# A depthwise-conv tile shared by two engines: GpSimd's 16 taps and VectorE's nine kept as two sums, value weights folded into the projection

## What is computed

```python
# block 1: linear attention over raw and convolved q, k, v
qkv = concat(h @ wq.T, h @ wk.T, h @ wv.T)            # 768 channels
dw  = depthwise_conv5x5(qkv, dw_kernel)               # 25 taps for each channel
pw  = grouped_conv1x1(dw, pw_kernel)                  # groups of 8 channels
f   = concat(qkv, pw).reshape(B, 64, 3 * 8, N)        # 64 heads of 8
query, key, value = relu(f[:, :, :8]), relu(f[:, :, 8:16]), f[:, :, 16:]
scores = einsum('bhdn,bhen->bhde', concat(value, 1), key)
out = einsum('bhde,bhen->bhdn', scores, query); out = out[:-1] / (out[-1:] + EPS)
x   = batchnorm(conv1x1(out, proj_kernel)) + x
# block 2: softmax attention over the 1024 pixels of each image
norm = (x - mean) / sqrt(var + EPS)
att  = softmax((f_w norm + f_b)^T (g_w norm + g_b))   # 1024 x 1024
x    = o_w (att applied to (h_w x + h_b)) + o_b + x
```

## Time and profile before

| what | value |
|---|---|
| median of 3 runs | 716.86 us (716.64 to 716.91) |
| the profiled execution: its own time | 716.49 us |
| its span, first to last instruction | 714.5 us |
| instructions in the span | 8764 |
| mean granted TensorE clock | 0.969 |
| one image in the middle | 153.9 us |

### The profile page before, as it was taken

One profiled execution on the slowest core, in us unless ns is written; L12 is line 12 of the kernel. 1 busy time (PEld: TensorE's weight loads), 2 busy tenths in 40 slices (PEclk: granted clock), 3 DMA queues, 4 the chain that ended last, 5 costly groups with the idle time before them and its releaser, 6 DMA issues.

```text
span 714.5 us, 8764 instructions
## 1 busy us (share of the span) xinstructions
PE 647.9 (91%) x3236; PEld 484.4 (68%) x3236; DVE 567.7 (79%) x661; ACT 470.0 (66%) x744; POOL 541.2 (76%) x253
## 2 busy tenths in 40 slices
PE   4979989999999999899999999899899946997998
PEld 3845458656767887657687886658678833485887
DVE  5899998879989999888899999888899982442221
ACT  4795529788676967978686697977688552232231
POOL 4999979899989998899989998999999790000000
PEclk9999999999999999999999999999999986898999
DMA  8000010001100000001100000000100000000000
GB/s 291 1 1 1 0 33 28 0 1 59 60 1 16 15 31 1 1 0 60 60 6 25 17 16 1 0 1 6 54 16 16 31 0 0 1 0 1 15 15 30
DMA packets 6538, 16.25 MB, mean 23 GB/s; under 512 B 864, under 2 KB 992, under 8 KB 5984
## 3 DMA queue, kind: packets, MB, share of 16 engines
q1 hardware_dynamic: 6496, 15.69, 6.0%
HBM read 11.50 MB, written 4.19 MB: 22 GB/s over the span
## 4 chain that ended last, share of the span: by engine, by line
PE 50%; DVE 19%; ACT 14%; POOL 12%; issue 4%; DMA 1%; POOLq 0%; SPq 0%; DVEq 0%; ACTq 0%
PE ps L614 13%; POOL rows L1318 12%; PE ps L590 12%; DVE ps L1107 11%; ACT prod L873 5%; PE ps L691 5%; PE ps L625 3%; PE ps L605 3%; DVE small L1244 2%; PE ps L739 2%; PE ps L533 2%; PE ps L456 1%; PE ps L665 1%; ACT kt L887 1%; ACT rows L1015 1%
## 5 line engine op out<-in xcount | busy, mean ns | idle before, releaser
L1318 POOL TENSOR_TENSOR conv<-conv,prod 128x930 f32<-128x930 f32 (+4 forms) x197 | 433.1, 2232 | 30.7 <-ACT prod L873 27.4
L1107 DVE SCALAR_TENSOR_TENSOR ps<-raw,dw_sb,ps 128x930 f32<-128x930 f32 (+4 forms) x295 | 354.1, 1200 | 7.7
L873 ACT ACTIVATE prod<-raw,dw_sb 128x930 f32<-128x930 f32 (+4 forms) x233 | 252.1, 1136 | 30.7 <-POOL conv L1318 18.1
L614 PE MATMUL ps<-ht,pt 128*128 128x256 f32 x512 | 115.1, 379 | 0.0
L614 PEld LDWEIGHTS ps<-ht,pt 128*128 128x128 f32 x512 | 95.1, 190 | 11.8
L1318 POOL TENSOR_TENSOR rows<-rows,prod 128x930 f32<-128x930 f32 (+4 forms) x36 | 83.0, 2306 | 14.1 <-ACT prod L873 9.3
L1015 ACT ACTIVATE rows<-ps,small 128x1024 f32<-128x1024 f32 x32 | 35.6, 1113 | 76.9 <-DVE small L1248 76.9
L1244 DVE TENSOR_REDUCE small<-ps 128x1 f32<-128x1024 f32 x32 | 39.0, 1220 | 33.0 <-PE ps L590 33.0
L590 PE MATMUL ps<-hi,t_hi 128*128 128x512 f32 x128 | 46.2, 444 | 13.1 <-ACT rows L1015 13.1
L887 ACT ACTIVATE kt<-ps 128x256 f32<-128x256 f32 x68 | 31.5, 466 | 23.4 <-PE ps L647 19.6
L590 PE MATMUL ps<-lo,t_hi 128*128 128x512 f32 x128 | 43.1, 420 | 0.0
(11 more groups left out here) (137 smaller groups left out, 1046.4 us busy)
## 6 DMA issues: line engine op xcount, KB each, us to landing
q_raw<-x_dram SPq DMA_DIRECT2D x8, 512.0 KB, 6.4
x<-x_dram SPq DMA_DIRECT2D x4, 1024.0 KB, 4.8
out_dram<-x_t SPq DMA_DIRECT2D x16, 256.0 KB, 2.3
conv<-wqkv_dram SPq DMA_DIRECT2D x1, 768.0 KB, 4.5
conv<-fg_dram SPq DMA_DIRECT2D x1, 512.0 KB, 5.3
proj_sb<-proj_dram SPq DMA_DIRECT2D x1, 512.0 KB, 7.5
pw_sb<-pw_dram SPq DMA_DIRECT2D x1, 384.0 KB, 6.4
mask_sb<-masks_dram SPq DMA_DIRECT2D x1, 264.0 KB, 6.1
```

The source lines that it names most:

```text
L614: mm = pe.matmul(dst[:, 0:C], pt[:, i % PT_BUFS, j, :], ht[:, j, :], start=(j == 0), stop=(j == NB - 1))
L873: act.activation(dst, view, ACT.Copy, scale=weight(t, i)).then_inc(prod_ready, 1)
L1107: return dve.scalar_tensor_tensor(dst, view, w, before, ALU.mult, ALU.add)
L1318: pool.tensor_tensor(total, total, product, ALU.add).then_inc(conv_pool, 1)
```

## The change

- POOL's part of tile 1 becomes one sum in `conv`: taps 0 to 15 (0 to 20 in the first image). The first seven stand among tiles 4 and 5, the last nine are the late ones. So tap 0 goes to `conv`, and there is no product into a row buffer.
- DVE's part becomes a sum of its own: taps 16 to 24 (21 to 24), starting with a plain product, the last tap writing to row buffer 2, now called `dve_part`. That tap waits for the transposes of the last softmax row in that buffer. DVE no longer waits for POOL's sum.
- PE multiplies `dve_part` first, then, after POOL's last add, `conv`.
- ACT may make three late products while the softmax loop of the last image still ends (`LATES_ATT`). The product buffers are counted through from image to image; before, the first five products of an image waited for all adds of the image before it.
- The pointwise weights of the value tiles are multiplied once, at the start, into the projection weights (two products on PE, one copy on ACT), and the value tiles of the key/value blocks are transposed instead of multiplied. The kernel's host side lays these weights out transposed, in the same array.
- The tables are written anew; POOL splits the second image's input after its early adds and not among them.

Line numbers in the changed kernel differ by some 10 to 20: L873 is L890, L1318 is L1336, L1107 is L1124, L1103 is L1120. The diff, cut:

```diff
-LATE = 10
-SHARED_TAPS, FIRST_SHARED_TAPS = 7, 12
+POOL_SHARED, FIRST_POOL_SHARED = 16, 21
+LATE = 9
...
-    for i in range(shared):
-        own.insert(SHARED_AT + 2 * i, (SHARED_TILE, LATE + i))
+    for i in range(shared - LATE):
+        own.insert(SHARED_AT + 2 * i, (SHARED_TILE, i))
+    own += [(SHARED_TILE, i) for i in range(shared - LATE, shared)]
...
+FIRST_POOL_SEQ = pool_order([tap for tap in ALL_TAPS if tap not in PE_TAPS], FIRST_POOL_SHARED)
+DVE_SEQ = [(t, i) for t in DVE_TILES for i in range(NTAPS) if (t, i) not in POOL_SEQ]
...
+FIRST_TAPS = (42, 49, 56, 63)
...
+LATES_ATT = (1, 2)
...
+PRODUCTS_X1T = (2, 0, 1, 1)
...
+        dve_part = rows[:, CK, :]
...
-                pe.wait_ge(conv_pool, add_count(b, POOL_ADDS))
+                pe.wait_ge(conv_pool, add_count(b, early_adds(b)))
                 for j in range(A_PWKV):
                     dst = a_slot(A_AT["pwkv", b] + j)
                     for t in range(CK, TILES):
-                        c0 = (t - CK) * P
-                        mm = pe.matmul(dst[:, c0:c0 + P], conv[:, t, j * P:(j + 1) * P], pw_sb[:, t, :],
-                                       start=True, stop=True)
+                        c0, block = (t - CK) * P, conv[:, t, j * P:(j + 1) * P]
+                        if t < 2 * CK:
+                            pe.matmul(dst[:, c0:c0 + P], block, pw_sb[:, t, :], start=True, stop=True)
+                        else:
+                            mm = pe.transpose(dst[:, c0:c0 + P], block, ident)
...
-                    mm = pe.matmul(dst, pw_sb[:, t, :], conv[:, t, cols], start=True, stop=(t != SHARED_TILE))
                     if t == SHARED_TILE:
+                        pe.matmul(dst, pw_sb[:, t, :], dve_part[:, cols], start=True, stop=False)
                         if h == 0:
-                            pe.wait_ge(conv_pool, late_add_count(b, LATE - 1))
-                        mm = pe.matmul(dst, pw_sb[:, t, :], late[:, cols], start=False, stop=True)
+                            pe.wait_ge(conv_pool, add_count(b, len(pool_adds(b))))
+                    mm = pe.matmul(dst, pw_sb[:, t, :], conv[:, t, cols], start=(t != SHARED_TILE), stop=True)
...
+            pe.wait_ge(fg_ready, 1)
+            for h in range(CK):
+                mm = pe.matmul(ps[:, 5, h * C:(h + 1) * C], pw_sb[:, 2 * CK + h, :], proj_sb[:, CK + h, :],
+                               start=True, stop=True)
+            mm.then_inc(value_weights_full, 1)
...
+                        index = add_count(b, adds.index((t, i)))
+                        if index >= PROD_BUFS:
+                            act.wait_ge(conv_pool, index - PROD_BUFS + 1)
+                        dst, part = product_buffer(index), True
...
+                    if i >= NB - 1 and with_next:
+                        n = LATES_ATT[i - NB + 1]
+                        if n:
+                            products(PRODUCTS)
+                            conv_products(b + 1, done[0], done[0] + n)
+                            done[0] += n
...
+            act.wait_ge(value_weights_full, 1)
+            act.copy(proj_sb[:, CK:2 * CK, :], ps[:, 5, :].rearrange("p (k m) -> p k m", k=CK)).then_inc(
+                value_weights_ready, 1)
...
-                    if i == NTAPS - 1 and b:
+                    if i == NTAPS - 1 and b and t == SHARED_TILE:
+                        dve.wait_ge(t_full, 16 * (b - 1) + 2 * (NB - 1))
+                    elif i == NTAPS - 1 and b:
                         dve.wait_ge(a_full, conv_read(b - 1, t))
-                    final = square(conv[:, t, :])
-                    if t == SHARED_TILE and i == shared:
-
-                        adds = ADD_SEQ if b else FIRST_ADD_SEQ
-                        done = adds.index((t, i - 1)) + 1
-                        if n >= DVE_TAPS - CARRY:
-                            done = POOL_ADDS if b else len(FIRST_ADD_SEQ)
-                        dve.wait_ge(conv_pool, add_count(b, done) if b else done)
-                        tap(acc, t, i, final).then_inc(conv_dve, 1 + skipped)
-                    else:
-                        starts = n == 0 or DVE_SEQ[n - 1][0] != t
-                        tap(final if i == NTAPS - 1 else acc, t, i, None if starts else acc).then_inc(conv_dve, 1)
+                    final = square(dve_part if t == SHARED_TILE else conv[:, t, :])
+                    starts = n == 0 or DVE_SEQ[n - 1][0] != t or skipped > 0
+                    tap(final if i == NTAPS - 1 else acc, t, i, None if starts else acc).then_inc(conv_dve, 1 + skipped)
...
-            conv_adds(0, FIRST_SPLIT, POOL_ADDS)
+            conv_adds(0, FIRST_SPLIT, early_adds(0))
             for b in range(B):
-                late_adds(b)
+                conv_adds(b, early_adds(b), len(pool_adds(b)))
...
+    pw_bd[:, 2 * CK:] = pw_bd[:, 2 * CK:].transpose(2, 1, 0).copy()
```

124 lines of the change are left out of this document (53 added, 71 removed).

## The result

| | before | changed |
|---|---|---|
| median, us | 716.75 (4 runs) | 702.48 (4 runs) |
| runs, us | 716.86, 716.64, 716.91, 713.19 | 702.30, 702.67, 702.01, 710.02 |
| ratio | | 0.9838, 95% interval 0.9805 to 0.9871 |
| profiled execution: own time, span, us | 716.49, 714.5 | 702.30, 700.5 |
| granted TensorE clock, mean over the span | 0.969 | 0.976 |

The kernel is 14.3 us faster. I forecast 4.65 us and a range that ends at 707.5. The direction was right, the size was wrong by a factor of three.

The account below looks back on a forecast made before the run. The prediction took PE to bound the kernel, so time counts only where PE is held up. First image -1.05, three images -2.1 and last image -1.5 sum to -4.65 us, from 716.49 to 711.8; predicted 712.0, range 707.5 to 716.5.

Parts of the forecast that it names:

- the transposes: Key/value blocks: transposes in place of half the matmuls have the same 128 columns, costed at nothing.
- the clock of the energy products: Second energy products after a PE wait: might move to full clock, 1.6 us for each of three images; rival, chance 0.12.
- First image: Start: denominators two DVE taps earlier, scaled queries one; -1.05 us, bounds 0 to 1.6 saved.
- the cover: First image: PE's 1.63 us wait takes up the about 1 us push from the added products and copy.
- Key/value blocks: Key/value stage of images 0 to 2: fewer ACT products between blocks; -0.7 us each, bounds 0.3 to 0.86.
- The wait for POOL: Turn of images 0 to 2: POOL gets ahead and PE's wait for its late sum goes; -0.58 us each.
- The fold: Images 0 to 2: one more ACT product ahead of the folded weights; +0.6 us on PE's path, bounds 0 to 1.
- Last image: Last image: DVE's sum 0.7 us sooner, PE's tile 1 products without a stop; -1.5 us, bounds -0.7 to -3.
- The slower one: Rival: transposes make the clock fall in the key/value blocks; 718.6 or 725.0 us, chance 0.09.
- The full product buffer: Rival: ACT waits for POOL's adds before a full product buffer, 4.5 of 4.65 us back; 716.7 us, chance 0.12.
- more gained: Rival: slow energy matmuls reach full clock and the fold's 0.6 us is hidden; 6.6 us more, 705.6 us, chance 0.12.

Follow-up runs that it names:

- fold_on_before: The kernel before with only the value-weights fold, including transposes in the key/value blocks and the product and copy at the start; 715.68 us, ratio 1.0007.
- no_early_lates: The changed kernel with the three late products of the softmax loop's end made behind the first key/value blocks again; 714.49 us, ratio 0.9981.
- late_fold_gap: The changed kernel with the value-weights product and copy made later, and one ACT product moved from ahead of the folded weights to behind them; 700.54 us.
- warm_before: The kernel before with matmuls of no use in PE's wait ahead of each image's second energy product; 710.68 us, ratio 0.9943.
- ident_matmul: The changed kernel with the value tiles' transposes in the key/value blocks made fp32 matmuls against the identity; 707.19 us, ratio 0.9883.
- best: The changed kernel with late value-weights copy, one ACT product moved, 17 shared taps in the last image, and useless matmuls in PE's waits; 691.12 us, ratio 0.9662.
- pad2_before: The kernel before with two 512-column matmuls of no use in front of the first image's key/value blocks; 717.28 us, ratio 1.0020.
- late_fold: The changed kernel with PE's value-weights product behind the raw queries and ACT's copy behind the second image's split; 704.06 us, ratio 0.9840.
- last_taps: The changed kernel with the late value-weights copy and 17 shared taps for GpSimd instead of 16 in the last image alone; 701.63 us, ratio 0.9808.

## Why the prediction was wrong, step by step

**What missed.** Two terms stand at nothing in the sum and measure 9.2 us together: the transposes (-3.0 us in three images) and the clock of the energy products (-6.2, four slow groups gone of five). The first is a step that I had wrong, the second a rival to which I gave 0.12. They turn the forecast's 711.8 into 702.6, and 702.30 was measured; the misses of the other terms nearly cancel. With the transposes alone it would have been 708.8, inside the range that ends at 707.5, and with the clock alone 705.6, outside. So it was the clock that carried the time out of the range.

**First image, -1.05: right for the taps, wrong for the cover.** The taps' new order is worth 1.23 us. The cover failed. I set the extra microsecond of PE and ACT against PE's 1.63 us wait for the denominators. But the chain goes PE, ACT, PE's scores, DVE, denominators. DVE takes the scores at a fixed place among its taps and had no slack there; what comes late to it makes everything behind it late, the denominators for which PE waits too. I had read who PE waits for and not who waits for PE. And the push was not 1 us: DVE's scores come 2.1 us later, 1.54 without the later input. So the change itself costs the start 0.3 us, and the input's 0.55 make it the measured +0.84.

**Key/value blocks, -0.7: near for the tables, wrong for the transposes.** The tables' part is 8.01 to 7.07 us, -0.94, a little over my bound of 0.86. The sentence that failed is "the transposes in place of half the matmuls have the same 128 columns, and I cost them at nothing". They are 1.8 us less PE work, of which 1.1 to 1.2 count. Half of the evidence stood in the earlier trace rows: 48 and 16 records for eight blocks of four matmuls, 64 for 32. The other half was the raw transposes' count in the same trace, one record each. I wrote "64 are 7.15 us" and took the records for the matmuls. This is the step of the working that failed: 0.5 us in image 0 and 1.2 to 1.3 in images 1 and 2. `fold_on_before` shows that only the tables let it count.

**The wait for POOL, -0.58: right in two images of three.** It is gone in images 1 and 2. In image 0 it stays: the trace lists 0.44 us before and 0.54 after. POOL's wait for the next image's first product did not go as I said, it grew from 1.17 to 2.59 us. And `no_early_lates` shows that POOL's lead was not what the early late products are for. ACT's room between the read-outs is: with 8 products there instead of 5, images 1 and 2 cost 2.7 and 3.0 us more, without a wait for POOL.

**The fold, +0.6: right**, measured +0.67 (1.36 against 0.69 us of wait), and `late_fold_gap` took it back.

**Last image, -1.5: right in its mechanism, too small in all.** DVE's sum came 0.71 us sooner (forecast 0.7), PE's second product 1.62 us (forecast 1.5 to 1.6). From there to the score transposes it is another 1.0 us, and that is the clock, which came back one pair of matmuls earlier (1.35 and 1.02 us for the last two pairs; before, 1.35 for the last alone). Behind it, one slow energy group less is 1.6 us of the 4.6. The last 0.4 us I have not traced.

**The rivals.** The slower one, a fallen clock in the blocks, did not happen in any profile. The full product buffer shows up as one wait of ACT of 0.79 to 0.85 us in the softmax loop of each image. PE's next wait for ACT is 0.83 us and was 0.73, so it costs 0.1 us at most. The rival "more gained" was the one that came true: its clock part, at 1.6 us for each of three images, happened as priced, and the last image lost one slow group too. Its other half, the fold hidden, did not happen. That I put this part at nothing and gave it 0.12 is the larger miss; what `warm_before` shows in its place is that the groups run at the full clock once PE is kept busy ahead of them, 1.55 us for each; why the change did the same in its profiled execution stays open.

The account of the 14.0 us of span, by the stages:

| part | us | from |
|---|---|---|
| start | +0.8 | first body; +0.55 of it is the later input |
| tables with the fold's wait | -2.7 | images of `warm_before` against `ident_matmul`: -0.3, -1.1, -1.3 |
| transposes | -3.0 | `ident_matmul` against the changed kernel: -0.5, -1.3, -1.2 |
| last image without the energies | -3.0 | -4.6 less 1.6; 1.0 of it is clock as well |
| slow energy groups, 5 to 1 | -6.2 | 1.55 to 1.6 each |

Rounding leaves 0.1. The one slow stretch of `ident_matmul` is taken off its third image. For a middle image, two parts of -1.2 and one of -1.55 make -3.95, and -3.97 was measured. The forecast's -0.7 stands against the first. By its own terms that one is -0.94 (blocks) - 0.58 (POOL) + 0.67 (fold) = -0.85, and another 0.34 is a wait that I had not read, ACT's at the raw key transposes (0.64 to 0.30 us): -1.19. Image 0 gains less, as PE waits there 0.52 us for ACT and 0.54 for POOL.

What stays open is why the kernel before had the slow groups in all three middle images in nearly all its executions (this is inferred from its clock, 0.966 to 0.969 in 22 of the 23 beside the first four kernels; its one profile shows three), and the changed one in some only. The runs show that PE's wait ahead of them is needed for it, and that a shift by 1.5 us doesn't stop it. They don't show what else decides.

## What to carry to other kernels

Count the records of an instruction group against the loop in the source before multiplying a duration: two records for one fp32 matmul and one for a transpose were the price list of this change. When a step is put on a chain that an engine waits for, ask at each engine on the chain where it has slack, and not only at the end of it. Where the bounding engine has a wait of a microsecond or more and a dense group behind it, look at the granted clock there; matmuls of no use in the wait took 4.6 us off one kernel (715.28 to 710.68). Off the other they took 7.9 by the medians (704.06 to 696.17), and 5.4 against its three executions at the better clock (701.1 to 701.9).

## What the runs showed of the hardware

- An fp32 matmul of 128x128 by 128 columns is two records of 0.11 us each at the full clock, a transpose of the same size is one. At the same place, the same data by a matmul against the identity: 7.31 us against 5.48 for eight blocks.
- PE's waits of 1.0 to 5.6 us can be followed by stretches at half clock. Added up from windows over the whole span, PE was granted half clock for 44.7 us before, 34.2 in the changed kernel and 20.5 in `best`. With filler in the waits, 15 us of the last image ran at 1.00 instead of 0.51 in the execution that was profiled.
- The middle images' slow groups differ between kernels and executions: three in the profiled executions of before, `fold_on_before` and `pad2_before`, none in those of the changed kernel, `late_fold`, `last_taps` and `late_fold_gap`; `ident_matmul` had one and `no_early_lates` two. In `best` and `late_fold_gap` one image has its slow stretch at the scores instead, behind a wait of 1.0 us for DVE or ACT. Executions of `late_fold` lie around 701.6 us with a mean clock of 0.976 and at 706.4 with 0.969. The mean clock doesn't tell all: executions of the kernel before at 0.969 lie between 713.4 and 716.9 us.
